# Two copies issued earlier in a one-core vision block: token transposes on ScalarE, a tile's expert weights on VectorE

## The reference, cut to what matters

```
h = tokenizer(x)                       # 3-level Haar, gated bands, inverse Haar
h = concat([cls_tok, h], axis=1)       # 257 tokens of 256 features, 8 images
h = h + attention_block(layernorm(h))  # 16 heads, 64 features, linear attention, MLP
h = h + moe(layernorm(h))              # router, top 2 of 8 experts

q_f, k_f = elu(q @ proj) + 1, elu(k @ proj) + 1
attn = q_f @ (k_f^T v) / (q_f @ sum(k_f))
out_e = silu(x @ w1[e] + b1[e]) @ w2[e] + b2[e]
```

## Time and profile before

| what | value |
|---|---|
| median of three timed runs | 739.04 us (737.57 to 739.18) |
| the profiled execution, its own time | 734.85 us |
| its span, first to last instruction | 733.0 us |
| mean granted TensorE clock | 0.966 |
| TensorE busy | 684.5 us, 93% |
| VectorE, ScalarE, POOL busy | 343.6, 293.7, 289.1 us |

### The profile page before, as it was taken

The page is one execution under the profiler, slowest core; times in us unless marked ns, Lnnn a source line. Parts: engine busy times, 40 slices in busy tenths (PEclk is TensorE's granted clock), DMA queues, the critical chain, the costliest instruction groups (busy, mean ns, idle before and its releaser), DMA issues.

```text
span 733.0 us, 14613 instructions
## 1 busy us (share of the span) xinstructions
PE 684.5 (93%) x4607; PEld 605.7 (83%) x4608; DVE 343.6 (47%) x1029; ACT 293.7 (40%) x762; POOL 289.1 (39%) x324
## 2 busy tenths in 40 slices
PE   0977999999999999999999999999999999999993
PEld 0755888889988877788888788999999999999993
DVE  5493766666532643654566554333333333333330
ACT  0432665466532363444345242333342424333330
POOL 7003677676662353444533332323232323232221
PEclk9978999999959999999999999999999999999997
DMA  9605999700000298011021253221221211122210
GB/s 210 221 2 97 271 303 307 207 0 1 2 0 1 82 377 289 16 45 45 23 81 59 96 183 94 37 43 30 44 34 30 34 34 30 30 36 37 36 22 0
DMA packets 53222, 63.97 MB, mean 87 GB/s; under 512 B 6348, under 2 KB 48768, under 8 KB 53008
## 3 DMA queue, kind: packets, MB, share of 16 engines
q1 hardware_dynamic: 41264, 50.61, 23.7%
q0 software_dynamic: 8112, 9.04, 7.4%
q10 hardware_dynamic: 3808, 3.82, 1.7%
HBM read 31.01 MB, written 31.38 MB: 85 GB/s over the span
## 4 chain that ended last, share of the span: by engine, by line
PE 73%; DVE 9%; SPq 5%; DMA 4%; issue 3%; ACT 2%; POOL 2%; DVEq 0%; POOLq 0%; ACTq 0%
PE bank L1702 70%; SPq L574 3%; DMA arena<-in_L_tok_Wa 2%; PE bank L2209 1%; DVE arena L1032 1%; DMA out_tokens<-h 1%; DMA h<-arena 1%; DVE small L549 1%; POOL small L570 1%; SPq L642 1%; PE bank L1734 1%; POOL arena L764 1%; PE bank L1880 1%; SPq L578 1%; DVE dense L562 1%
## 5 line engine op out<-in xcount | busy, mean ns | idle before, releaser
L1702 PE MATMUL bank<-arena,dense 128*128 (+2 forms) x1408 | 307.0, 389 | 1.1 <-ACT arena L1496 0.8
L1702 PEld LDWEIGHTS bank<-arena,dense 128*128 128x128 f32 (+1 forms) x1408 | 247.2, 193 | 37.1 <-ACT arena L1595 2.9
L1671 ACT ACTIVATE dense<-bank,small 128x128 f32<-128x128 f32 x320 | 91.1, 368 | 182.5 <-PE bank L1702 182.5
L857 POOL DMA_INDIRECT out_tokens<-dense,slot_ids x40 | 77.1, 1928 | 206.1 <-DVE dense L1415 197.4
L1702 PEld LDWEIGHTS bank<-dense 128*128 128x128 f32 x1280 | 149.0, 192 | 3.9 <-DVE dense L1393 2.0
L1702 PE MATMUL bank<-dense 128*128 128x128 f32 x1280 | 149.6, 275 | 1.6 <-DVE dense L1393 1.6
L1702 PE MATMUL bank<-dense,arena 128*128 128x256 f32 (+2 forms) x688 | 105.2, 352 | 1.1 <-ACT arena L1509 0.7
L764 POOL TENSOR_TENSOR arena<-arena 128x512 f32<-128x512 f32 x64 | 80.3, 1277 | 40.7 <-ACT arena L1529 40.7
L1702 PEld LDWEIGHTS bank<-dense,arena 128*128 128x128 f32 (+2 forms) x688 | 81.8, 186 | 16.3 <-issue 4.2
L1595 ACT ACTIVATE arena<-bank,small 128x256 f32<-128x256 f32 x128 | 53.7, 471 | 81.7 <-PE bank L1702 81.5
L1702 PE MATMUL bank<-arena 128*128 128x34 f32 (+7 forms) x756 | 81.8, 301 | 3.1 <-ACT arena L1595 1.6
(11 more groups left out here) (247 smaller groups left out, 580.1 us busy)
## 6 DMA issues: line engine op xcount, KB each, us to landing
routed_rows<-x SPq DMA_DIRECT2D x8, 2385.0 KB, 24.3
arena<-in_L_ffn_w SPq DMA_DIRECT2D x13, 1024.0 KB, 12.5
dense<-routed_rows SPq DMA_DIRECT2D x40, 132.5 KB, 2.1
arena<-in_L_ffn_w ACTq DMA_DIRECT2D x3, 1024.0 KB, 9.4
arena<-in_x SPq DMA_DIRECT2D x4, 512.0 KB, 7.0
arena<-in_L_attn_w SPq DMA_DIRECT2D x2, 1024.0 KB
out_tokens<-h SPq DMA_DIRECT2D x8, 256.0 KB, 2.2
h<-arena SPq DMA_DIRECT2D x13, 128.0 KB
```

The lines of the kernel that those rows point to most:

```text
L857: pool.indirect_dma_start(out=sums[:, :], out_offset=bass.IndirectOffsetOnAxis(ap=slot_ids[par][:, 0:1], axis=0), in_=y[par], in_offset=No ...
L1671: act.activation(hT[par][:, k, :], psUP[par][c][:, P * m:P * m + P], ACT.Silu, bias=b1now[par][:, k:k + 1]).then_inc(hT_sb, 1)
L1702: return pe.matmul(out, lhsT, rhs, start=start, stop=stop, **kw)
```

## The change

Two pieces of order change, and no arithmetic.

1. ScalarE's copy of the transposed tokens of image g+2 (`tokens_T(g + 2, par)`) moves from behind bank 5 to behind the key copy, ahead of bank 4 and bank 5. It waits there for TensorE's transposes as it did before.
2. VectorE computes the second part of the table in step 2, after `weights_in(4)` and ahead of `rows_in(3)` and `tile_out(2)`. The weights of the fifth tile (tile 4) are so copied before the table and no longer behind it. Steps 2 and 3 are peeled from the loop for that, which now starts at step 4.

```
@@ vector
                 if isinstance(i, int) and i == 0:
                     settle(B - 1, 1)
+                if isinstance(i, int) and i == 2:
+                    tables(False)
                 if not isinstance(i, int) or i + 1 < MOE_TILES:
                     rows_in(i + 1, 1 - par, turns + par)
                 tile_out(i, par)
-            expert_step(0, 0, 1)
-            expert_step(1, 1, 1)
-            tables(False)
+            for i in range(4):
+                expert_step(i, i % 2, i // 2 + 1)
 
             def turn(it):
-                expert_step(2 * it + 2, 0, it + 2)
-                expert_step(2 * it + 3, 1, it + 2)
-            chain.loop(MOE_TILES // 2 - 2, 2, turn)
+                expert_step(2 * it + 4, 0, it + 3)
+                expert_step(2 * it + 5, 1, it + 3)
+            chain.loop(MOE_TILES // 2 - 3, 2, turn)
@@ scalar
                 bank_out(3)
                 if not peeled or g + 1 < B:
                     k_T(g + 1, 1 - par)
+                if not peeled or g + 2 < B:
+                    tokens_T(g + 2, par)
                 bank_out(4)
                 bank_out(5)
-                if not peeled or g + 2 < B:
-                    tokens_T(g + 2, par)
                 bank_out(6)
```

## The result

| | kernel before | changed kernel |
|---|---|---|
| median, timed side by side | 738.9 us (18 runs, 734.75 to 743.55) | 734.27 us (18 runs, 730.41 to 737.53) |
| ratio after/before | | 0.9938 [0.9918, 0.9958] |
| profiled execution, own time | 734.85 us | 733.56 us |
| its span, mean granted clock | 733.0 us, 0.966 | 731.7 us, 0.966 |

The changed kernel is faster, by 4.6 us or 0.6%. The two profiled executions differ by 1.3 us only, less than a third of what the medians say. That is the first thing to explain.

The account below looks back on a forecast made before the run. TensorE carries 73% of the chain, so only its waits can be won: 1.4 us (token copy) + 0.8 us (weights of tile 4) = 2.2 us off 739.04, forecast 736.8 us, range 734.0 to 739.2.

Parts of the forecast that it names:

- Part 1, the token copy: Attention steps: the copy fits in ScalarE's idle time and TensorE's four waits for it go, 1.4 us gained.
- The high end is the 1.4, which is all there is: Attention steps: moving the token copy can gain at most the 1.4 us of TensorE's waits for it.
- loop steps should be 17.5 us apart: Sign in the changed kernel's profile: attention loop steps follow each other every 17.5 us at full clock.
- Part 2, the weights of tile 4: Experts: TensorE's 1.62 us wait at tile 4 goes, a new 0.80 us wait comes at tile 5; 0.8 us gained.
- The sum: Whole kernel: 1.4 us from the token copy and 0.8 from the weights, 2.2 us in all, forecast 736.8 us.
- the first rival: Attention step 3: the fall of the clock, costing 1.7 us, goes with the 0.35 us gap; 735.1 us, chance 0.22.
- I carry the difference over as it is: The profiled execution lay 4.2 us under the median; the 2.2 us gain was taken off the median 739.04 unchanged.
- The second rival: Experts, tile 5: late rows eat nearly all the gain from the weights, leaving 0.1 us; 737.5 us, chance 0.13.
- The third: Experts, tile 4: VectorE's weight copy waits 1.34 us for POOL's DMA; 0.9 us gained in all, 738.1 us, chance 0.04.
- The fourth rival: Attention: bank 4 starts late in all steps, so moving the token copy gains nothing; 738.2 us, chance 0.07.
- The fifth: Attention: the clock falls in two more stretches, each costing 1.7 us; 740.2 us, slower than before, chance 0.06.
- by more than one: Whole kernel: clock falls differing by over one in number or length would mean the clock, not the order, made the time.

Follow-up runs that it names:

- e4: The changed kernel, unchanged, timed again as a control: 734.50 us, ratio 0.9946 to the kernel before.
- e5: The changed kernel with the token copy put back behind bank 5 in loop steps 1 and 3: 736.6 us, ratio 0.9966 to the kernel before.
- e3: The kernel before, unchanged, timed again as a control: 740.49 us, ratio 1.0013.
- e8: The kernel before with the token copy moved one bank later, behind bank 6: 748.32 us, ratio 1.0124.
- e1: The kernel before with the token copy moved alone, the table left in its old place: 736.96 us, ratio 0.9967.
- e9: The changed kernel, unchanged, timed again beside other kernels: 733.83 us, ratio 0.9934 to the kernel before.
- e11: The changed kernel, unchanged, timed once more beside other kernels: 733.54 us, ratio 0.9925 to the kernel before.
- e2: The kernel before with only the table moved behind the weights of tile 4, the token copy in its old place: 738.57 us, ratio 0.9992.
- e7: The changed kernel with its second table cut in two, the rest run in step 3 behind the weights of tile 5: 732.39 us, ratio 0.9909 to the kernel before.
- e10: The changed kernel with its second table cut in two, timed a second time: 732.45 us, ratio 0.9900 to the kernel before.

## Why the prediction was right, and where it was not

**What bounds the kernel.** Right: TensorE's waits were the place to look, and the changed kernel gains exactly where they stood.

**Part 1, the token copy.** The mechanism held: the copy went into ScalarE's idle time, all four waits went, bank 4 of step 0 started 0.52 us behind the end of the transposes (80.55 to 81.07) where it had been 0.18, and that cost nothing to be seen, and no instruction of POOL or ScalarE took their place as TensorE's releaser in steps 1 to 5. The size was off. "The high end is the 1.4, which is all there is" is wrong: each wait costs its bracket and 0.17 us of lost overlap, so four are worth 1.4 + 0.7 = 2.1 us. The same loss is missing from "loop steps should be 17.5 us apart": they are 17.33.

**Part 2, the weights of tile 4.** Held in its order and nearly in size. `rows_in(3)` came 8.05 us behind the end of `tile_out(1)` (449.15 to 457.20) where it had been 7.93 (449.69 to 457.62), 0.1 later and not 0.2. The rows landed 10.64 us behind that end (459.79), the forecast 10.66 (460.35). TensorE however was 0.28 us nearer to that end than before: its transposes of tile 4 stood 2.17 us behind it (451.32) and had stood 2.45 behind (452.14). It asked that much sooner and waited 1.06 us instead of 0.80. In the other profiles of this order the wait was 1.17 (e4) to 1.87 us (e5), and the old wait at tile 4, 1.62 in the profile read, was 2.04 in e3, 2.17 in e8 and 2.24 in e1. From the transposes of tile 4 to those of tile 5 it is 9.14 us before (452.14 to 461.28) and 8.47 after (451.32 to 459.79): 0.67 gained, where the forecast had 0.82. Of this 0.2 is lost again: the next transposes follow after 7.44 us in the changed kernel and after 7.25 before. Up to tile 6 it is 16.39 us before (16.94 in e3) and 15.91 after (16.18 in e4, 16.27 in e9, 16.20 in e11), so part 2 is worth about 0.5 us.

**The sum: two terms that it had too small.** 2.2 us were forecast and 4.6 measured. That the time still lay inside the range is owed to the room left for the first rival, not to the sum. The step that was off in the order is "the high end is the 1.4", by the 0.7 us of lost overlap. The larger one is the clock: the sum has it at nothing, and leaves it to the first rival. By the terms that the profiles show the gain is:

- order: 2.1 (copy) + 0.5 (weights) = 2.6 us, where the prediction had 2.2;
- clock: the one fall that goes with the gap of step 3, 1.7 us, where it had nothing.

That makes 4.3 us; 4.6 were measured, with an interval of 3.1 to 6.1. The timed runs have the clock term about as large: the mean clock is 0.9616 in the 78 runs of the kernel before that were timed beside the experiments (0.958 to 0.967) and 0.9638 in the 21 of the changed kernel (e4, e9, e11), 0.0022 more. One fall is worth 1.7 us, half of its 3.4 us, or 0.0023 of the mean clock.

A difference in mean clock can't be turned into time without knowing where it lies, though. Among the 78 runs of the kernel before, the time goes down by only some 0.4 us for each 0.001 of mean clock (a fitted line), while a fall in the loop steps costs 0.74 for the same (1.7 for 0.0023). One reason shows in the profiles: late in attention there is a longer stretch of low clock, 17.07 us in nine profiles and 13.65 in four, and in it TensorE waits for POOL (L764): from L1880/L1881 of step 6 to that of step 7 it is 18.97 to 19.00 us in all thirteen.

"I carry the difference over as it is" did no harm, since the 2.2 us were taken off the median. But the profile read was not a typical execution: it had one fall in steps 0 to 5 where e3 and e2 had three, and two falls are 3.4 of the 4.2 us by which it lay under the median; e3's profiled execution, which has them, took 738.58 us. The falls that it lacked are in both kernels; the one that it had is the one that the change took away.

**The first rival** (0.22) is what happened. A fall directly behind the 0.35 us gap, or its longer successor in e8, was in step 3 in all five profiles that have the gap there (before, e3, e2, e5, e8) and in none of the eight that don't. I had held two things against it. One was that no fall followed the longer gap of step 1; that is still unexplained. A fall did come there in e3, e2 and e5, but also in after, e4, e9 and e11, which have no gap in that place. The other was phase.

TensorE: Matmul & The Clock Gate, "What's actually happening", of the Trainium skill has the monitor's window run free of the kernel. For falls in steps 0 to 2, which come and go between executions of the same kernel (none in before and e7, two in e3 and e10), the traces agree. For step 3, five of five against none of eight, phase from one execution to the next is not what decided.

What in the gap decides is not shown. The fall began 0.11 to 0.61 us behind the start of L1880/L1881 of step 3 in all five. A gap takes idle time into that stretch and also makes everything behind it later; no run has the one without the other, and the fall of e10 in step 2 needed no gap.

**The others.** The second rival, rows that eat all of part 2 by a wait of 1.50 us, was passed only by e5's 1.87; the four profiles of the changed kernel have 1.06, 1.17, 1.39 and 1.32, all above the 0.80 of the forecast. The third is refuted: the copy at 450.24 ran its usual 1.23 us inside POOL's DMA issue of 450.01 to 451.59. The blocking that SBUF — State Buffer, "Who interferes with whom", of the Trainium skill describes did not hold it. Another copy was longer: the one two tiles later took 1.53 us inside a DMA issue of POOL of 2.17 us. Whether the one stretches the other is not shown.

```profile
466.20 2.17 POOL L857 DMA_INDIRECT out_tokens<-dense,slot_ids  x1 [4.92 <-DVE dense L1415]
...
466.75 1.53 DVE L1393 COPY dense<-arena 128x2048 f32 x1 [1.42 <-issue]
```

No matmul of TensorE waited for it. The fourth rival is refuted by the waits. The fifth, more falls, happened in reverse.

**What would have shown it.** The prediction named the right thing to look at, but its bound was too coarse: falls that differ "by more than one". The whole effect is one fall. In this one pair the count even differed the wrong way, one in steps 0 to 5 before and two after, and only the repeated profiles showed that step 3's fall goes with the order of the kernel and the others with the execution.

**Open:** why the gap of 0.61 us in step 1 brought no fall in the first profile and no additional one in the others, and 0.35 in step 3 did; whether the idle time of a gap or the shift that it gives decides; and how much of the clock term lies outside step 3. Behind the long gap at tile 4 or 5 there was a fall in e1, e5 and e8 and none in the other profiles, e3 with its wait of 2.04 us among them. So part 2 may save falls too; no run shows it by itself. The clearest is e1 (TensorE's timeline):

```profile
457.96 5.46 PE L1702 MATMUL bank<-dense 128*128 128x128 f32 x32 [2.24 <-DVE dense L1393]
```

The same 32 matmuls take 3.73 us at full clock at 454.99 above.

## What to carry to other kernels

Price a wait of TensorE by the distance between the same instruction in two neighbouring periods, not by the bracket alone, and look at the granted clock of the stretch behind it: here the bracket of 0.35 us in step 3 was worth 0.35 + 0.17 + 1.7 us. Before two profiles are compared, count the falls of the clock in each and take more than one profile of each kernel: here one execution had one fall in attention and the next three. A mean clock alone doesn't give the time, since a fall where TensorE waits for another engine anyway costs next to nothing. The long chain of small instructions on VectorE was cheaper in two pieces, each shorter than the slack of what was queued behind it.

## What the hardware showed that was not expected

- A TensorE wait in the attention steps cost 0.17 us beyond its idle time (17.33 us for a step without it, 17.49 net of it), in each pair of profiles compared.
- The granted clock fell to 0.50 for 3.4 us behind a gap of 0.35 us, with TensorE busy for 17.5 of the 17.8 us before it, in each of the four profiles that had this gap in step 3. A fall was also seen with no gap at all (e10, step 2).
- A low clock where TensorE waits for another engine cost next to nothing: 18.97 to 19.00 us from step 6 to step 7, with 13.65 us of low clock around it or 17.07.
- Of thirteen profiles only e7's has no such fall in steps 0 to 5; it has the highest mean clock, 0.970, and the shortest time of a profiled execution, 729.73 us.
- VectorE's copy of 128x2048 took 1.23 us inside one DMA issue of POOL (450.24) and 1.53 inside another (466.75).
